# Turning and splitting the second layer's weights behind the first unit of a graph and expert kernel, through two PSUM banks

## The reference, cut to what matters

```
x = x + gnn(layernorm(x), adj, Wl, bl, Ws, bs, Wr, br, ln_w, ln_b)   # two layers
x = x + ffn(layernorm(x), ...)                                       # routed experts
# one layer of gnn, h is 128 samples of 128 x 384:
u = h @ h.T / sqrt(384);  delta = softmax(u) * adj
attn = delta / (sum(delta) + 1e-10)
ctx = (attn * upper) @ (h @ wl.T + b_l) + diag(attn) * (h @ ws.T + b_s)
    + (attn * lower) @ (h @ wr.T + b_r)
h = relu(layernorm(ctx) * g + beta)
```

## Time and profile before

| what | us |
|---|---|
| median of three runs | 2161.67 |
| lowest and highest | 2161.18, 2163.12 |
| the profiled execution | 2160.51 |
| its span in the profile | 2158.7 |
| PE busy in the span | 2091.0 (97%) |
| DVE, ACT, POOL busy | 1656.5 (77%), 1491.7 (69%), 1413.0 (65%) |

### The profile page before, as it was taken

The page is one execution under the profiler, slowest core; times in us unless marked ns, Lnnn a source line. Parts: engine busy times, 40 slices in busy tenths (PEclk is TensorE's granted clock), DMA queues, the critical chain, the costliest instruction groups (busy, mean ns, idle before and its releaser), DMA issues. The chain is left out here.

```text
span 2158.7 us, 56998 instructions
## 1 busy us (share of the span) xinstructions
PE 2091.0 (97%) x13580; PEld 2038.0 (94%) x13581; DVE 1656.5 (77%) x5452; ACT 1491.7 (69%) x3901; POOL 1413.0 (65%) x3348
## 2 busy tenths in 40 slices
PE   6999999999999999999999999999999999968997
PEld 5999999999999999999999999999999999957996
DVE  5777777777777777677777777777777777758997
ACT  4777767667776776676776776677776767637775
POOL 2556666666666666666666666666666666655887
PEclk9999999999999999999999999999999999978999
DMA  7101111211111111111111111111111111117995
GB/s 194 32 27 50 38 49 48 104 50 47 43 49 50 51 42 50 43 47 47 43 46 50 47 42 50 44 50 50 50 39 50 47 39 49 34 56 234 279 294 192
DMA packets 94261, 153.77 MB, mean 71 GB/s; under 512 B 17621, under 2 KB 70619, under 8 KB 93954
## 3 DMA queue, kind: packets, MB, share of 16 engines
q1 hardware_dynamic: 75844, 99.61, 16.0%
q0 software_dynamic: 17408, 50.62, 6.1%
q10 hardware_dynamic: 704, 0.10, 0.0%
HBM read 96.11 MB, written 57.32 MB: 71 GB/s over the span
## 5 line engine op out<-in xcount | busy, mean ns | idle before, releaser
L422 PE MATMUL bank<-wT_hi,hT_hi 128*128 128x384 f32 x2304 | 798.8, 347 | 11.3 <-issue 4.8
L424 PE MATMUL bank<-wT_hi,hT_lo 128*128 128x384 f32 x2304 | 774.2, 336 | 0.0
L423 PE MATMUL bank<-wT_lo,hT_hi 128*128 128x384 f32 x2304 | 773.1, 336 | 0.0
L422 PEld LDWEIGHTS bank<-wT_hi,hT_hi 128*128 128x128 f32 x2304 | 434.9, 189 | 20.5 <-ACT bank L622 12.4
L423 PEld LDWEIGHTS bank<-wT_lo,hT_hi 128*128 128x128 f32 x2304 | 435.2, 189 | 0.0
L424 PEld LDWEIGHTS bank<-wT_hi,hT_lo 128*128 128x128 f32 x2304 | 434.0, 188 | 0.0
L1173 POOL TENSOR_TENSOR hT_lo<-hT,hT_hi 128x384 fp32r<-128x384 f32 x256 | 261.5, 1022 | 22.9 <-ACT hT_hi L687 21.3
L682 ACT ACTIVATE hT<-bank 128x384 f32<-128x384 f32 x256 | 125.9, 492 | 203.0 <-PE bank L414 183.5
L658 ACT CAST right_hi<-bank 128x384 fp32r<-128x384 f32 x256 | 122.6, 479 | 173.9 <-PE bank L424 173.2
L1228 POOL TENSOR_SCALAR_AFFINE_SELECT deltaT_hi<-turned_hi 128x128 fp32r<-128x128 f32 x256 | 85.3, 333 | 211.8 <-ACT turned_hi L664 209.2
L414 PE MATMUL bank<-hT 128*128 128x128 f32 x1536 | 213.3, 275 | 0.0
(11 more groups left out here) (201 smaller groups left out, 5145.2 us busy)
## 6 DMA issues: line engine op xcount, KB each, us to landing
tok<-buckets SPq DMA_DIRECT2D x72, 388.0 KB, 4.5
x_in<-in_x_dram SPq DMA_DIRECT2D x128, 192.0 KB, 2.5
x_res<-in_x_dram SPq DMA_DIRECT2D x128, 192.0 KB, 2.4
adj_in<-in_adj_dram SPq DMA_DIRECT2D x128, 64.0 KB, 2.4
buckets<-pads SPq DMA_DIRECT2D x9, 388.0 KB, 4.9
out_dram<-out_rows,row_ids POOLq DMA_INDIRECT x144
buckets<-rows,dest_words POOLq DMA_INDIRECT x128, 2.7
w_top<-in_L_ffn_w_dram SPq DMA_DIRECT2D x2, 768.0 KB
```

What stands on the lines that cost most here:

```text
L422: pe.matmul(o, hi, w_hi, start=False, stop=False, skip_group_check=True)
L423: pe.matmul(o, hi, w_lo, start=False, stop=False, skip_group_check=True)
L424: last = pe.matmul(o, lo, w_hi, start=False, stop=(c == C - 1), skip_group_check=True)
```

## The change

The first layer's nine pieces are turned and split where they were. The second layer's nine move behind unit 0: on PE between `aggregate` of unit 0 and `make_router`, on ACT and DVE to the empty second half of step 0. They no longer go through three banks but through two, bank 6 and bank 1, alternating. The first two pieces wait for unit 0's `low_deltaT`, each later one for the split of the piece two before it. Since bank 6 is overwritten by them, PE opens it again afterwards, and ACT's `self_term` of unit 1 waits for that. `open_banks` waits for nine pieces only. SP's code is unchanged: its wait for 18 turned pieces still stands ahead of the expert weights.

```diff
+            late_banks = (bank[1], bank[6])
+
+            def weight_bank(n):
+
+                return weight_banks[n % 3] if n < 3 * C else late_banks[n % 2]
...
                                 n = (l * 3 + m) * C + dc
-                                if n >= 3:
+                                if l == 0 and n >= 3:
                                     pe.wait_ge(wT_lo_made, n - 2)
+                                if l == 1 and n < 3 * C + 2:
+                                    pe.wait_ge(deltaTlo_ready, 1)
+                                elif l == 1:
+                                    pe.wait_ge(wT_lo_made, n - 1)
                                 for oc in range(C):
-                                    last = pe.transpose(weight_banks[n % 3][:, oc * P:(oc + 1) * P],
+                                    last = pe.transpose(weight_bank(n)[:, oc * P:(oc + 1) * P],
                                                         stage[:, m, l, oc, dc * P:(dc + 1) * P], ident[:])
                                 last.then_inc(wT_done, 1)
...
-                        pe.wait_ge(wT_lo_made, 3 * C * L)
-                        pe.wait_ge(wT_hi_made, 3 * C * L)
+                        pe.wait_ge(wT_lo_made, 3 * C)
+                        pe.wait_ge(wT_hi_made, 3 * C)
...
                             if u and isinstance(i, int) and i == 0:
+                                turn_weights(1)
+                                pe.wait_ge(wT_lo_made, 3 * C * L)
+                                pe.wait_ge(wT_hi_made, 3 * C * L)
+                                pe.matmul(ctx_banks[1][:, 0:D], ident_r[:], wT_hi[:, 0, 0, 0, :], start=True, stop=True
+                                          ).then_inc(opened, 1)
                                 make_router()
...
-                    for l in range(L):
-                        turn_weights(l)
+                    turn_weights(0)
...
+                        elif n == 1:
+                            act.wait_ge(opened, 2)
                         act.activation(ctx_banks[odd][:, 0:D], self_bank[:, 0:D], ACT.Copy,
...
+                            if isinstance(i, int) and i == 0 and half == 1:
+                                high_weights(1)
...
-                    for l in range(L):
-                        high_weights(l)
+                    high_weights(0)
...
+                            if isinstance(i, int) and i == 0 and half == 1:
+                                low_weights(1)
...
-                    for l in range(L):
-                        low_weights(l)
+                    low_weights(0)
```

More of the change, by code:

```diff
@@ L727, in high_weights @@
                                 act.wait_ge(wT_done, n + 1)
-                                act.copy(wT_hi[:, l, m, dc, :], weight_banks[n % 3][:, 0:D]).then_inc(wT_hi_made, 1)
+                                act.copy(wT_hi[:, l, m, dc, :], weight_bank(n)[:, 0:D]).then_inc(wT_hi_made, 1)
                     def step(i, key):
@@ L884, in low_weights @@
                                 dve.wait_ge(wT_hi_made, n + 1)
-                                dve.tensor_tensor(wT_lo[:, l, m, dc, :], weight_banks[n % 3][:, 0:D],
+                                dve.tensor_tensor(wT_lo[:, l, m, dc, :], weight_bank(n)[:, 0:D],
                                                   wT_hi[:, l, m, dc, :].bitcast(F32),
```

## The result

The changed kernel takes 2172.11 us (median of five runs, 2169.47 to 2174.49) where the kernel before takes 2161.67. The ratio is 1.0047, with a 95% interval of 1.0036 to 1.0059: slower by 0.36 to 0.59%. The forecast was 2173.5 us, 0.55%.

A forecast was written before the change was run, and what follows sets the result against it. PE, busy 97% of the span, was taken to bound the kernel. Unit 3's +10.3 us and the clock's +1.5 made +11.8: 2160.51 became 2172.3, and with the median 1.16 above, 2173.5 us; range 2168 to 2176.5.

The forecast's parts named there:

- The front, -5.1 us: Ahead of all units: `open_banks` waits for fewer turned pieces and starts at 20.97 in place of 26.10.
- The pieces behind unit 0, 7.2 to 9.1 us to the eighteenth: On PE after `aggregate`: nine pieces through two banks, middle 8.1 us from start to the eighteenth turned piece.
- SP's eight loads, and the adjacency 19.0 us behind them: In SP's queue: expert loads start at 42.1 and sample 2's adjacency lands behind them at 61.1.
- The chain of 6.6 us to unit 3: On DVE and ACT, from unit 2's masked sums to unit 3's first product: 6.6 us, bounds 6.3 to 7.3.
- So unit 3, +10.3 us: On PE: unit 3 starts at 67.7 in place of 57.41, bounds +7.1 to +12.0.
- The clock, +1.5 us: On PE: an added 1.5 us for half-speed clock, expected between 60 and 71 us.
- After standing several microseconds in unit 2 PE will meet this again: On PE behind unit 2's wait: the clock falls to half speed again, counted at 1.5 us.
- the shift ahead of the stand: Before DVE wants sample 2's adjacency in unit 2: work arrives 3.4 to 5.5 us later than before.
- the stand: At unit 2's masked sums: DVE waits some 7 us for sample 2's adjacency.
- The adjacency does not wait: In the DMA queue: sample 2's adjacency passes the expert weights; +3.4 us (2165.1) or +5.5 (2167.2); chance 0.13.
- PE's clock stays low: On PE: half clock through the pieces and a long run behind unit 2's wait; +14.7 us, 2176.4; chance 0.12.
- Faster: Behind unit 0: pieces cost less than half their round, so the kernel takes at most 2157 us; chance 0.03.

The follow-up runs named there:

- Experiments 2: The changed kernel with SP's wait ahead of the expert weights for the first layer's nine pieces only; median +8.8 us on the kernel before, ratio 1.0031 to 1.0065.
- experiment 3: The changed kernel with sample 4's rows and sample 2's adjacency issued ahead of SP's wait; median +9.1 us on the kernel before, ratio 1.0026 to 1.0058.
- experiment 4: The kernel before with SP's expert-weight wait moved to unit 0's low part of the turned attention; D10 (distance at unit 10) +6.3 us.
- Experiment 6: The changed kernel with SP's nine-piece wait plus 37 unread products on PE; median +5.8 us on the kernel before, ratio 1.0007 to 1.0032.
- experiment 7: The changed kernel with SP's nine-piece wait and second-layer pieces between unit 0's products through three banks; 2222.38 us against 2226.35 for the kernel before.
- experiment 8: Late pieces between unit 0's products, SP's wait for all eighteen put back; median 0.0 us from the kernel before, ratio 0.9985 to 1.0006.
- experiments 1: The changed kernel unaltered, run again on another chip; median +8.1 us on the kernel before, ratio 1.0028 to 1.0055.

## Why the prediction was right, point by point

*The front, -5.1 us.* Held: from the first transpose to `open_banks` it was 26.10 - 13.69 = 12.4 us and is 21.61 - 14.32 = 7.3. DVE's wait for sample 2's rows showed, with 0.84 us, and cost nothing, as said.

*The pieces behind unit 0, 7.2 to 9.1 us to the eighteenth.* Held: 34.68 to 42.35, 7.7 us (8.1 was taken). The rounds were the faster ones, 1.65 to 1.71 us; the last piece was turned at half clock. The router started after 9.3 us (8.5 to 10.6 was given).

*SP's eight loads, and the adjacency 19.0 us behind them.* Held: 42.38 to 48.49 + 12.8 = 61.3, 18.9 us; the forecast had the landing at 61.1. Experiments 2, 3 and 4 show it from three sides: remove the late wait, move the two loads ahead of it, or bring it into the kernel before.

*The chain of 6.6 us to unit 3.* From the landing at 61.3 to 67.59 it was 6.3, the lower bound.

*So unit 3, +10.3 us.* In the time of the span it came at 67.59 in place of 57.41, +10.2, but 0.6 of this is that the first transpose started later (14.32 in place of 13.69), which no term foresaw. Counted from the first transpose it came after 53.27 us in place of 43.72: +9.6. That 67.59 stands so close to the 67.7 of the forecast is in part luck: the later start (+0.6) makes up for the shorter turning (-0.4) and chain (-0.3).

*The clock, +1.5 us.* This is the term that was wrong in place and in size. The step "After standing several microseconds in unit 2 PE will meet this again" failed: PE had its 18 products of unit 2 until shortly before the landing (57.87 to 61.1), stood for 0.65 us and was then idle in small portions, and the clock stayed at full. Where PE did stand, for 3.64 us in experiment 4, the clock did fall, so that the step was right in kind; but it cost some 0.6 us there and not 1.5. What happened instead is that it fell during the pieces and stayed low over the router (4.1 us in place of 2.9) and unit 1 up to unit 2's first product (9.8 in place of 8.5), so that the shift ahead of the stand was 6.7 us and not 3.4 to 5.5, and the stand 5.45 us and not some 7. Experiment 6 prices this fall at 2.6 to 3.2 us where no stand covers it. The prediction saw that a longer fall in unit 1 "falls into the time before the adjacency lands, and costs nothing": since unit 3's start hangs on the landing, the sum did not move, only its parts. Without the extra term of 1.5 the forecast would have been 2172.0; that this is the measured 2172.11 owes something to the luck named above.

That is also why removing the stand gives back only 3.0 us: of the 9.6 us, -5.1 is the front, +9.3 the pieces, +2.4 the slower router and unit 1 (4.1 in place of 2.9, 9.8 in place of 8.5), and the last 3.0 the stand. I had held it for the larger part.

*The rivals.* "The adjacency does not wait": excluded, it landed as computed, and without the loads ahead of it it took 2.2 us (experiment 3). "PE's clock stays low": half right; the clock stayed low over 13 us, but where the landing covered it. "Faster": rightly held to be out of reach for pieces behind unit 0; experiment 7 shows that it was in reach for pieces beside it, with SP's wait moved as well; with that wait left as it was (experiment 8) the medians show no difference.

The rule of the Trainium skill that was weighed, that completions of one issuing engine need not come in order (DMA: Bandwidth & Descriptors, Queues, rings and completion order), may hold in general; for this transfer no run shows it. Issued 5.6 to 15 us behind the first expert load, it landed 19.0 us behind that load's issue before, 18.9 in the changed kernel, 19.1, 19.0 and 17.8 in experiments 1, 4 and 8, and 20.2 to 20.5 in the five runs in which SP waited for nine pieces only; the expert weights themselves were there 17.8 us behind it in experiment 3.

## What to carry to other kernels

A piece of work that is moved takes its completion semaphore along: look for every queue that waits for it, and for everything that is queued behind that wait on the same issuer, and ask when each of these is needed. Here one unedited wait on SP made a small transfer of the third unit stand behind 3.1 MB. And moving set-up work off the front pays only if it lands beside something: behind unit 0 a piece cost a bank's round (0.84 us and more), between products only its own transposes (0.33 us).

## What the runs showed that was not expected

The clock fell to half during the two-bank pieces; PE was busy for 1.02 and 1.27 of 2.00 us in the two stretches before. The same pieces through three banks kept it until they were done, at the front (1.85 of 2.00 us from 20 to 22 in the kernel before) and behind unit 0 (1.77 of 2.00 us from 38 to 40 in the run with three banks). It came back only 6 us after unit 1's products had started at 48.1; in the kernel before it took 4 us (42.05 to about 46.3). Filling the gaps with unread products kept it at full.

The clock column is not to be trusted for the first turning. One transpose of the first layer took 421 ns in the kernel before (median, 13.7 to 16.9 us), one of the second 273 ns; behind unit 0 in the changed kernel it took 273 ns at full clock and 418 at half. So the first layer's pieces went at the pace of half clock, while the profile has 1.00 for those stretches. That is what the prediction had as the slower pace.

The same kernel's expert part took 220.6 us on one chip and 283.4 on another, at 294 and 228 GB/s in its fastest slice, while the part ahead of it agreed within 0.2 us in 1934. Why was not tried.
